# Expert weights of a block fetched by SyncE with the expert's number in a register, in place of an indirect transfer from GpSimd, with the order planned anew

## The chip, the cores and the metric

One core of a Trainium2 chip runs the kernel. Its engines are TensorE (PE for matmuls, PEld for weight loads), VectorE (DVE), ScalarE (ACT), GpSimd (POOL) and SyncE (SP), and 16 DMA engines move data for all of them. The metric is the device time in microseconds (us) of one execution; the times shown are medians over runs.

## The reference, cut to what matters

The input is 64 sequences of 128 tokens with 128 features, beside a context of 77 rows for each. Four layers follow one another: a transformer layer (self-attention, cross-attention, MLP), a layer with two attentions and a mixture of experts, a state-space block with cross-attention, and a last masked cross-attention with a norm. The change touches the mixture of experts alone:

```python
logits = h @ rw.T + rb                      # 8 experts
vals, idx = top_k(logits, 2)
gates = softmax(vals)
h1 = gelu(einsum('nd,efd->enf', hf, fc1_w) + fc1_b)   # D=128 -> FF=512, per expert
eo = einsum('enf,edf->end', h1, fc2_w) + fc2_b        # back to 128
mixed = (eo[idx, n] * gates).sum over the 2 chosen experts
return x + mixed
```

## The kernel before, in words

The 64 sequences are worked off in 16 passes of four sequences (NB = 4). Four streams (S = 4) are in flight at once, each with its own buffers; stream n does passes n, n+4, n+8 and n+12. A pass is a list of several hundred steps (`pass_steps`), each on one to three engines one after the other.

**What sets the order.** Every engine does its steps strictly in one order that is worked out before the kernel is built. `timetable` plays all four streams through with a length for each step (`parts`, in us, such as `"place": [(P, 0.9), (V, 5.0)]`), rules of priority (`EAGER`, `AHEAD`, `LEAD`, `STAY`) and a table `CHANGES` that overrides these rules for each stretch of planned time (`STRETCH`). Out of it come, for each engine, its list of steps (`pl.order`), the PSUM banks, and the order in which the passes hold the one set of expert slots (`pl.holders`). On the chip only this order counts: an engine that comes to a step waits on semaphores until its inputs are there, and everything behind it on that engine waits too.

**The mixture of experts.** The step `route` makes the logits, `pick` (L1655 to L1666, DVE) ranks them, `place` counts on PE (L1289 to L1293) and works out on DVE (L1674 to L1698) the row of each token in a list that is sorted by expert and padded to 15 blocks of 128 rows, and the expert of each block. `scatter` (L1850) writes the tokens to their rows in HBM with eight indirect DMAs from POOL. `sorted` (L1116, SP) reads the blocks back, `sort_turn` turns them. Then, for each of the 15 blocks j, `up` (L1307 on PE, L1705 on DVE, L1503 on ACT) and `down` (L1314 on PE, L1712 on DVE) use the weights in slot j % 4 of the tile `ew`. `put` (L1120, SP) writes the answers back, and `get` (L1869) gathers them with eight indirect DMAs from POOL.

**The weights of a block.** One expert is 128 rows of 4,624 bytes in the HBM tensor `experts`, 592 KB in all. `ew` has four slots. The step `fetch` (L1852 to L1863) is done 15 times a pass by POOL: it waits until `place` is done, and until the slot is free: for blocks 0 to 3 until the former holder's last `down`, from block 4 on until `down` of block j - 4. Then it issues an indirect DMA whose 128 row numbers stand in `expert_row`:

```python
g_.indirect_dma_start(ew[:, j % SLOTS, :], None, experts,
                      bass.IndirectOffsetOnAxis(expert_row[s][:, j:j + 1], 0))\
    .then_inc(experts_fetched[j % SLOTS], 16)
```

POOL also spreads the keys of every attention (L1880), works on every norm's statistics (L1811 to L1821), adds biases (L1840), and does parts of the state-space block. SP does nothing but wait and issue: `load` (L1095 to L1097), `context` (L1113), `sorted`, `put`, `store` (L1144).

Of the kernel before, what the change touches and what calls it, by code (L numbers as in the profile page):

```python
# [32 lines left out]
I32 = mybir.dt.int32  # L33
# [7 lines left out]
NE = 8  # L41
# [6 lines left out]
SLOTS = 4  # L48
# [159 lines left out]
def pe(n, count=1):  # L208

    return count * (0.006 + 0.00167 * n)  # L210
# [7 lines left out]
INDIRECT = 1.1  # L218


def parts(step):
# [50 lines left out]
    if kind == "out":  # L272
# [176 lines left out]
def timetable(streams):  # L449
# [106 lines left out]
    while True:  # L556
# [52 lines left out]
STRETCH = 80  # L609
CHANGES = [  # L610
    {"LEAD": 1.24415, "mix": {P: -0.7}},
    {"LEAD": 1.24415, "values": {P: 8.9, V: 0.5}, "soft": {V: 0.7}, "mix": {P: -0.7}, "pick": {V: -1.7},
     "scatter": {G: -3.8, Y: -3.8}, "scan": {V: -1.3}},
    {"LEAD": 1.24415, "STAY": 0, "values": {P: 8.9, V: 0.5}, "soft": {V: 0.7}, "mix": {P: -0.7}, "pick": {V: -1.7},
     "place": {V: 0.2}, "scatter": {G: -3.8, Y: -3.8}, "step_size": {P: 1.5}, "decay_in": {G: 20.8},
     "scan": {V: -1.3}, "gate_norm": {G: 2.7}},
    {"LEAD": 1.24415, "STAY": 0, "apply": {A: -0.6}, "values": {P: 8.9, V: 0.5}, "soft": {V: 0.7}, "mix": {P: -0.7},
     "pick": {V: -1.7}, "place": {V: 0.2}, "scatter": {G: -3.8, Y: -3.8}, "step_size": {P: 1.5},
     "decay_in": {G: 20.8}, "scan": {V: -1.3}, "gate_norm": {G: 2.7}},
    {"LEAD": 1.24415, "STAY": 7.88007854, "apply": {A: -0.6}, "values": {P: 8.9, V: 0.5}, "soft": {V: 0.7},  # L620
     "mix": {P: -0.7}, "pick": {V: -1.7}, "place": {V: 0.2}, "scatter": {G: -3.4, Y: -3.8}, "step_size": {P: 1.5},
     "decay_in": {G: 20.8}, "scan": {V: -1.3}, "gate_norm": {G: 2.7}},
    {"LEAD": 1.24415, "STAY": 2.24318536, "apply": {A: -0.6}, "values": {P: 8.9, V: 0.5}, "spread": {G: -1},
     "soft": {V: 0.7}, "turn": {P: 1.8, A: 1.8}, "mix": {P: -0.7}, "pick": {V: -1.7}, "place": {V: 0.2},
     "scatter": {G: -3.4, Y: -3.8}, "step_size": {P: 1.5}, "decay_in": {G: 20.8}, "scan": {V: -1.3},
     "gate_norm": {G: 2.7}},
    {"LEAD": 1.24415, "STAY": 2.24318536, "apply": {A: 1.7}, "values": {P: 8.9, V: 0.5}, "spread": {G: 0.7},
     "soft": {V: 0.7}, "turn": {P: 1.8, A: 1.8}, "mix": {P: -0.7}, "pick": {V: -1.7}, "place": {V: 0.2},
     "scatter": {G: -3.4, Y: -3.8}, "combine": {V: -1.4}, "step_size": {P: 1.5}, "decay_in": {G: 20.8},
     "scan": {V: -1.3}, "gate_norm": {G: 2.7}},  # L630
    {"LEAD": 1.24415, "STAY": 2.24318536, "apply": {A: 1.7}, "values": {P: 8.9, V: 0.5}, "spread": {G: 0.7},
     "soft": {V: 0.7}, "turn": {P: 1.8, A: 1.8}, "mix": {P: -0.7}, "pick": {V: -1.9}, "place": {V: 0.2},
     "scatter": {G: -3.4, Y: -3.8}, "combine": {V: -1.4}, "step_size": {P: 1.5}, "decay_in": {G: 20.8},
     "scan": {P: 6.5, V: 5.2, G: 5.3}, "gate_norm": {G: 2.7}},
    {"LEAD": 2.75006599, "bias_mlp": {G: -2.3}, "combine": {V: -2.2}},
    {"STAY": 7.7079338, "weigh": {G: -1.4}, "scan": {V: -1.2}},
    {"LEAD": 2.60550174, "STAY": 7.7079338, 5: 0.2, "apply": {A: -0.3}, "mlp": {V: 0}, "sort_turn": {P: 1.2, A: 1.9},
     "conv": {P: 1.1, V: 1.1, A: 1.2}, "weigh": {G: -1.4}, "scan": {V: -1.2}},
    {"LEAD": 2.60550174, "STAY": 7.7079338, 5: 0.2, "apply": {A: -0.3}, "mlp": {V: 0}, "sort_turn": {P: 1.2, A: 1.9},
     "conv": {P: 1.1, V: 1.1, A: 1.2}, "weigh": {G: -1.4}, "scan": {V: -1.2}, "mamba_out": {P: -3.7, V: -2.6}},  # L640
    {"LEAD": 2.60550174, "STAY": 7.7079338, 5: 0.2, "apply": {A: -0.3}, "mlp": {V: 0}, "place": {P: 1, V: 1},
     "sort_turn": {P: 1.2, A: 1.9}, "conv": {P: 1.1, V: 1.1, A: 1.2}, "weigh": {G: -1.4}, "scan": {V: -1.2},
     "gate_stats": {G: -0.1}, "mamba_out": {P: -3.7, V: -2.6}},
    {"LEAD": 2.60550174, "STAY": 1.47055777, 5: 0.2, "apply": {A: -0.3}, "mlp": {V: 0}, "place": {P: 1, V: 1},
     "sort_turn": {P: 1.2, A: 1.9}, "get": {Y: -1.2}, "conv": {P: 1.1, V: 1.1, A: 1.2}, "weigh": {G: -1.4},
     "scan": {V: -1.2}, "gate_stats": {G: -0.1}, "mamba_out": {P: -3.7, V: -2.6}},
    {"LEAD": 2.60550174, "STAY": 1.47055777, 5: 0.2, "apply": {A: -0.3}, "values": {P: 11.8}, "mlp": {V: 0},
     "place": {P: 1, V: 1}, "fetch": {G: -1.5, Y: -1.6}, "sort_turn": {P: 1.2, A: 1.9}, "get": {Y: -1.2},
     "step_size": {V: 5.1}, "conv": {P: 1.1, V: 1.1, A: 1.2}, "weigh": {G: -1.4}, "scan": {V: -1.2},
     "gate_stats": {G: -0.1}, "mamba_out": {P: -3.7, V: -2.6}},  # L650
    {"LEAD": 1.28926663, "STAY": 1.47055777, 5: 0.2, "apply": {A: -0.3}, "values": {P: 11.8}, "mlp": {V: 0},
     "place": {P: 1, V: 1}, "fetch": {G: -1.5, Y: -1.6}, "sort_turn": {P: 1.2, A: 1.9}, "get": {Y: -1.2},
     "step_size": {V: 5.1}, "conv": {P: 1.1, V: 1.1, A: 1.2}, "weigh": {G: -1.4}, "scan": {V: -1.2},
     "gate_stats": {G: -0.1}, "mamba_out": {P: -3.7, V: -2.6}},
    {"LEAD": 2.44299045, "STAY": 1.47055777, 5: 0.2, "apply": {A: -0.3}, "values": {P: 11.8}, "mlp": {V: 0},
     "place": {P: 1, V: 1}, "fetch": {G: -1.5, Y: -1.6}, "sort_turn": {P: 1.2, A: 1.9}, "get": {Y: -1.2},
     "step_size": {V: 5.1}, "conv": {P: 1.1, V: 1.1, A: 1.2}, "weigh": {G: -1.4}, "scan": {V: -1.2},
     "gate_stats": {G: -0.1}, "mamba_out": {P: -2.1, V: -2.6}},
    {"LEAD": 2.64227556, "STAY": 1.47055777, 5: 0.2, "apply": {A: -0.3}, "values": {P: 11.8}, "mlp": {V: 0},
     "place": {P: 1, V: 1}, "fetch": {G: -1.5, Y: -1.6}, "sort_turn": {P: 1.2, A: 1.9}, "get": {Y: -1.2},  # L660
     "step_size": {V: 5.1}, "conv": {P: 1.1, V: 1.1, A: 1.2}, "weigh": {G: -1.4}, "scan": {V: -1.2},
     "gate_stats": {G: -0.1}, "mamba_out": {P: -2.1, V: -2.6}},
    {"LEAD": 2.64227556, "STAY": 3.99262594, 5: 0.2, "apply": {A: -0.3}, "values": {P: 11.8}, "mlp": {V: 0},
     "place": {P: 1, V: 1}, "fetch": {G: -1.5, Y: -1.6}, "sort_turn": {P: 1.2, A: 1.9}, "get": {Y: -1.2},
# [1344 lines left out]
```

## Time and profile before

| | |
|---|---|
| median of 3 runs | 4012.08 us (4009.76 to 4013.83) |
| the profiled execution | 4007.73 us, its span 4005.9 us |
| mean granted clock of TensorE | 0.934 |
| busy: PE / DVE / ACT / POOL | 3432.5 / 2796.4 / 2686.8 / 1476.8 us |

An engine's busy time is the time in which it has an instruction of the program at work; waits, register work and the issuing of DMAs by SP are not counted. "remote", or "another core or an unknown queue", stands in this single-core trace where a semaphore came that no recorded instruction explains; "issue" is time in which an engine waited for nothing that the trace shows.

### The profile page before, as it was taken

Reading aid. Unit: us, or ns where it says so; the run is one execution under the profiler, and the core shown is the slowest. Engines: PE = TensorE matmul, PEld = TensorE weight load, DVE = VectorE, ACT = ScalarE, POOL = GpSimd, SP = SyncE. Lnnn points to the kernel's source line nnn. Section 1 sums busy time; section 2 is a strip of 40 time slices with the busy share of each in tenths; the row PEclk is TensorE's granted clock in tenths of the full one; section 3 lists DMA queues with packets and bytes.
Section 4 is the critical chain, followed back from the end, with each engine's and each line's share of the span. In section 5 each row is a group of like instructions: output and inputs, shape, how many; then the busy total and the mean of one; then the engine's idle time right before and its main releaser. Section 6 shows DMA issues by size and latency. Waiting matters only on the chain.

```text
span 4005.9 us, 86421 instructions
## 1 busy us (share of the span) xinstructions
PE 3432.5 (86%) x31600; PEld 2472.8 (62%) x31600; DVE 2796.4 (70%) x5826; ACT 2686.8 (67%) x4726; POOL 1476.8 (37%) x1844
## 2 busy tenths in 40 slices
PE   6888888889988979898988998988889798988776
PEld 3556656666656766575765765666566565756654
DVE  7777565757776766876767676776877667675554
ACT  3777665657867857696676766857667575767544
POOL 2123334434243343524334342343433425342441
PEclk9999998989999989999999989999899898999888
DMA  4000223121101221121111201221012211202210
GB/s 149 2 3 20 88 81 97 54 76 48 38 18 57 66 82 50 48 74 40 60 52 42 81 11 58 65 81 50 10 57 71 82 46 48 79 11 95 90 57 6
DMA packets 144378, 224.40 MB, mean 56 GB/s; under 512 B 20128, under 2 KB 106080, under 8 KB 143712
## 3 DMA queue, kind: packets, MB, share of 16 engines
q0 software_dynamic: 42752, 158.86, 12.4%
q1 hardware_dynamic: 101216, 60.02, 5.2%
q8 instruction: 265, 4.34, 0.5%
q14 instruction: 145, 1.19, 0.1%
HBM read 190.52 MB, written 36.98 MB: 57 GB/s over the span
## 4 chain that ended last, share of the span: by engine, by line
PE 49%; DVE 21%; ACT 13%; issue 6%; another core or an unknown queue 5%; POOL 3%; DMA 1%; SPq 1%; DVEq 0%; ACTq 0%; POOLq 0%
PE ps L1231 11%; PE ps L1243 6%; PE ps L1221 6%; DVE mx L1616 5%; DVE pr L1622 3%; ACT pt L1461 3%; PE ps L1307 3%; PE ps L1314 3%; PE ps L1190 3%; PE ps L1251 2%; PE ps L1216 2%; DVE kx L1755 2%; DVE kx L1622 2%; PE ps L1263 2%
## 5 line engine op out<-in xcount | busy, mean ns | idle before, releaser
L1616 DVE TENSOR_REDUCE mx<-ps 128x8 f32<-128x616 f32 (+1 forms) x704 | 671.5, 954 | 479.4 <-PE ps L1221 350.3
L1461 ACT ACTIVATE pt<-ps 77x512 f32<-77x512 f32 (+1 forms) x1408 | 769.4, 592 | 167.8 <-PE ps L1231 112.9
L1231 PE MATMUL ps<-k_sb,pr 128*77 128x128 f32 (+1 forms) x3776 | 564.6, 292 | 42.0 <-issue 12.4
L1231 PEld LDWEIGHTS ps<-k_sb,pr 128*77 128x77 f32 (+1 forms) x3776 | 442.5, 153 | 162.1 <-issue 98.9
L1243 PE MATMUL ps<-pt,v 77*16 77x128 f32 (+2 forms) x11264 | 471.1, 284 | 69.4 <-ACT pt L1461 33.7
L1452 ACT ACTIVATE pr<-pr 128x616 f32<-128x616 f32 (+1 forms) x472 | 394.8, 840 | 175.3 <-DVE pr L1622 165.4
L1880 POOL TENSOR_TENSOR kx<-kT,in_tiles 128x308 f32<-128x308 f32 (+1 forms) x384 | 317.4, 827 | 514.5 <-PE ps L1221 416.8
L1470 ACT ACTIVATE og<-ps 128x256 f32<-128x256 f32 x704 | 263.8, 377 | 299.1 <-PE ps L1243 174.2
L1622 DVE TENSOR_TENSOR pr<-ps,mx 128x616 f32<-128x616 f32 (+1 forms) x472 | 450.3, 954 | 16.2
L1221 PE MATMUL ps<-kx,qT 32*128 32x308 f32 (+2 forms) x2816 | 378.1, 570 | 82.4 <-ACT pt L1461 38.1
L1861 POOL DMA_INDIRECT ew<-experts,expert_row x240 | 238.8, 995 | 534.0 <-DVE kx L1712 440.1
L1243 PEld LDWEIGHTS ps<-pt,v 77*16 77x16 f32 (+2 forms) x11264 | 254.9, 99 | 275.1 <-issue 122.4
L1231 PE MATMUL ps<-k_sb,kx 128*77 128x128 f32 (+1 forms) x1856 | 280.4, 293 | 23.4 <-ACT og L1470 7.9
L1307 PE MATMUL ps<-pr,ew 128*128 128x128 f32 x1920 | 262.7, 281 | 23.0 <-DMA ew<-experts,expert_row 9.3
L1251 PE MATMUL ps<-k_sb,og 128*128 128x128 f32 x1408 | 234.7, 290 | 45.1 <-ACT og L1470 18.7
L1231 PEld LDWEIGHTS ps<-k_sb,kx 128*77 128x77 f32 (+1 forms) x1856 | 217.9, 153 | 85.8 <-issue 51.2
L1314 PE MATMUL ps<-ew,pt 128*128 128x128 f32 x1920 | 262.5, 281 | 8.7 <-ACT pt L1503 5.1
L1411 ACT ACTIVATE xh<-x,dt_p,rstd 128x128 f32<-128x128 f32 x448 | 183.9, 483 | 118.8 <-POOL dt_p L1821 118.7
L1307 PEld LDWEIGHTS ps<-pr,ew 128*128 128x128 f32 x1920 | 237.6, 194 | 41.7 <-issue 20.0
L1452 ACT ACTIVATE kx<-kx 128x616 f32<-128x616 f32 (+1 forms) x232 | 194.7, 840 | 100.9 <-DVE kx L1622 87.5
L1314 PEld LDWEIGHTS ps<-ew,pt 128*128 128x128 f32 x1920 | 236.9, 194 | 28.4 <-issue 16.5
L1251 PEld LDWEIGHTS ps<-k_sb,og 128*128 128x128 f32 x1408 | 164.7, 147 | 132.7 <-issue 53.1
(200 smaller groups left out, 6001.9 us busy)
## 6 DMA issues: line engine op xcount, KB each, us to landing
kx<-sorted_x SPq DMA_DIRECT2D x16, 960.0 KB, 9.1
sorted_y<-kx SPq DMA_DIRECT2D x48, 256.0 KB
x<-x SPq DMA_DIRECT2D x16, 256.0 KB, 3.2
experts<-weights SPq DMA_DIRECT2D x2, 2048.0 KB, 18.5
out<-xh SPq DMA_DIRECT2D x16, 256.0 KB, 2.5
sorted_x<-weights SPq DMA_DIRECT2D x4, 960.0 KB, 10.2
ew<-experts,expert_row POOLq DMA_INDIRECT x240
sorted_y<-kx SPq DMA_DIRECT2D x16, 192.0 KB
```

Of the source, the lines that this page charges most:

```text
L1221: i = mm(o, qT[s][r, b * L:(b + 1) * L], spread_keys[s][r, pl.slot(("spread", a, s, b), 2), 0:4 * keys], start=mask is None, stop=True)
L1231: i = tr(p[0:keys, j * L:(j + 1) * L], probs[s][pl.slot(unit, 3)][:, c:c + keys], ident)
L1243: i = mm(ps[32 * j:32 * j + t.slot, pl.banks[step][0], q * L:(q + 1) * L], heads_of(s, t)[0:keys, n, :], pt[s][0:keys, q, j * L:(j + 1) * ...
L1251: i = tr(p[:, q * L:(q + 1) * L], og[:, s % S, q * L:(q + 1) * L], ident)
L1307: i = mm(p[:, c * 128:(c + 1) * 128], E(j % SLOTS, "fc1", c * 128, (c + 1) * 128), blocksT[s][:, j * 128:(j + 1) * 128], start=True, stop= ...
L1314: i = mm(p[:, 0:D], h1[s][j % 2][:, c * 128:(c + 1) * 128], E(j % SLOTS, "fc2", c * D, (c + 1) * D), start=c == 0, stop=c == FC - 1)
L1452: go_act(v, v, ACT.Exp, scale=t.scale).then_inc(probs_ready.sem, 1)
L1461: go_act(pt[s][0:keys, q % 2, :], p[0:keys, :], ACT.Copy).then_inc(probsT_ready.sem, 1)
L1470: go_act(og[:, s % S, 2 * h * L:2 * (h + 1) * L], p[:, 0:2 * L], ACT.Copy)\
L1616: link(v_.tensor_reduce(m, tile, AX.X, ALU.max, negate=True))
L1622: tell(dve, v_.tensor_tensor(dst, tile, m.rearrange("p (c h) -> p c h", c=2).unsqueeze(3).broadcast_to([128, 2, 4, keys]), ALU.add), score ...
L1880: tell(pool, g_.tensor_tensor(spread_keys[s][:, pl.slot(step, 2), 0:4 * keys].rearrange("p (h k) -> p h k", h=4), kT[s][:, b * keys:(b + 1 ...
```

## The change

The step `fetch` goes from POOL to SP. `place` leaves the expert's number itself in a new tile `expert_id` in place of 128 row numbers. SP waits for the same four things as POOL did, loads the number from SBUF into a register, and issues an ordinary DMA whose source address is worked out from it. The tile `row_n` goes, with the one instruction that made it. In the planner, `fetch` is now one part on SP, the lengths of several steps are changed, `STRETCH` goes from 80 to 60, and `CHANGES` is a new table (60 stretches in place of 46), so the order of the steps on all five engines is a new one. No other instruction of the kernel differs.

```diff
-INDIRECT = 1.1
+INDIRECT = 1.03
...
     if kind == "fetch":
-        return [(G, INDIRECT), (Y, 3.4)]
+        return [(Y, 3.8)]
...
     if kind == "sorted":
-        return [(Y, 5.0)]
+        return [(Y, 7.5)]
     if kind == "put":
-        return [(Y, 3.0)]
+        return [(Y, 3.5)]
...
-        "pick": [(V, 1.9)], "place": [(P, 0.9), (V, 5.0)], "combine": [(V, 2.5)],
+        "pick": [(V, 2.5)], "place": [(P, 1.8), (V, 3.3)], "combine": [(V, 2.5)],
...
-        "up": [(P, pe(128, 4) + 0.02), (V, 0.72), (A, act(n))], "down": [(P, pe(D, 4) + 0.04), (V, 0.3)],
+        "up": [(P, pe(128, 4) + 0.07), (V, 0.72), (A, act(n))], "down": [(P, pe(D, 4) + 0.06), (V, 0.3)],
...
-STRETCH = 80
+STRETCH = 60
 CHANGES = [
...
@@ SyncE's steps
+                elif kind == "fetch":
+                    j = step[2]
+                    former = pl.holder(EXPERTS, s)
+                    sp.wait_ge(packed, 16 * 4)
+                    sp.wait_ge(*placed(s))
+                    if j >= SLOTS:
+                        sp.wait_ge(*down_ready(s, j - SLOTS))
+                    elif former is not None:
+                        sp.wait_ge(*down_ready(former, BLOCKS - 1))
+                    e = sp.value_load(expert_id[s][0:1, j:j + 1], min_val=0, max_val=NE - 1)
+                    sp.dma_start(ew[:, j % SLOTS, :], experts[bass.ds(e * 128, 128), :])\
+                        .then_inc(experts_fetched[j % SLOTS], 16)
@@ VectorE's preparation and the end of place
-            nc.vector.tensor_reduce(row_n[:], K("after"), AX.X, ALU.add)
...
-                    tell(dve, v_.scalar_tensor_tensor(expert_row[s][:], expert, 128.0, row_n[:].broadcast_to([128, BLOCKS]),
-                                                      ALU.mult, ALU.add), placed, s)
+                    tell(dve, v_.tensor_scalar(expert_id[s][:], expert, 0.0, None, ALU.add), placed, s)
@@ GpSimd's steps
-                elif kind == "fetch":
-                    s, j = args
-                    former = pl.holder(EXPERTS, s)
-                    pool.wait_ge(packed, 16 * 4)
-                    pool.wait_ge(*placed(s))
-                    if j >= SLOTS:
-                        pool.wait_ge(*down_ready(s, j - SLOTS))
-                    elif former is not None:
-                        pool.wait_ge(*down_ready(former, BLOCKS - 1))
-                    g_.indirect_dma_start(ew[:, j % SLOTS, :], None, experts,
-                                          bass.IndirectOffsetOnAxis(expert_row[s][:, j:j + 1], 0))\
-                        .then_inc(experts_fetched[j % SLOTS], 16)
```

## Rows read from the trace of the kernel before

**Rows 1.** The page: busy time of each engine, share of the span, instructions.
```profile
PE 3432.5 (86%) x31600; PEld 2472.8 (62%) x31600; DVE 2796.4 (70%) x5826; ACT 2686.8 (67%) x4726; POOL 1476.8 (37%) x1844
```

**Rows 2.** The page: the chain that ended last, share of the span by engine.
```profile
PE 49%; DVE 21%; ACT 13%; issue 6%; another core or an unknown queue 5%; POOL 3%; DMA 1%; SPq 1%; DVEq 0%; ACTq 0%; POOLq 0%
```

**Rows 3.** Busy time by stretch, sum of eight stretches without indirect DMAs, 658 us.
```profile
sum 658.00, PE 590.31 PEld 409.55 DVE 540.65 ACT 442.70 POOL 276.54; mean PE 73.79 PEld 51.19 DVE 67.58 ACT 55.34 POOL 34.57
```

**Rows 4.** The same, six stretches inside the work on blocks, 644 us.
```profile
sum 644.00, PE 603.13 PEld 451.99 DVE 481.18 ACT 514.67 POOL 238.61; mean PE 100.52 PEld 75.33 DVE 80.20 ACT 85.78 POOL 39.77
```

**Rows 5.** The same, eight stretches of 12 us from 4 us after a scatter's start, fetches behind.
```profile
sum 96.00, PE 40.75 PEld 26.28 DVE 33.01 ACT 21.58 POOL 73.81; mean PE 5.09 PEld 3.28 DVE 4.13 ACT 2.70 POOL 9.23
```

**Rows 6.** The same, nine stretches of 10 us from 4 us after a lone get's start.
```profile
sum 90.00, PE 49.84 PEld 30.48 DVE 27.66 ACT 26.93 POOL 50.25; mean PE 5.54 PEld 3.39 DVE 3.07 ACT 2.99 POOL 5.58
```

**Rows 7.** Timeline of all engines, 384 to 404 us: start, length, instruction, idle time before it.
```profile
384.76 1.23 POOL L1850 DMA_INDIRECT sorted_x<-xh,token_row  x1 [9.08 <-DVE expert_row L1698]
...
395.14 0.98 POOL L1861 DMA_INDIRECT ew<-experts,expert_row  x1 [0.30 <-issue]
...
397.69 0.80 DVE L1616 TENSOR_REDUCE mx<-ps 128x8 f32<-128x616 f32 x1 [6.90 <-remote]
...
402.01 0.38 ACT L1470 ACTIVATE og<-ps 128x256 f32<-128x256 f32 x1 [12.76 <-remote]
```

**Rows 8.** The tile `ew`: its fetch (ns min/median/max), and who waited for it (us, times).
```profile
L1861 POOL DMA_INDIRECT ew<-experts,expert_row x240: 932/979/1306, 395.1 to 3828.7; - x120
...
  PE ps L1307: 9.3, 9
```

**Rows 9.** Waits of all engines, us in total, times, longest.
```profile
POOL ew L1861 <- DVE kx L1712: 440.1, 100, 34.4
POOL kx L1880 <- PE ps L1221: 416.8, 93, 20.1
```

**Rows 10.** The longest pieces of the chain that ended last: start, length.
```profile
571.84 5.74 DMA ew<-experts,expert_row
...
2003.10 6.75 DMA ew<-experts,expert_row
...
2228.32 4.42 DMA ew<-experts,expert_row
```

**Rows 11.** DMA queues (packets, MB, share) and issues (count, KB, us to landing).
```profile
q8 instruction: 265, 4.34, 0.5%
...
kx<-sorted_x SPq DMA_DIRECT2D x16, 960.0 KB, 9.1
...
w_sb<-weights SPq DMA_DIRECT2D x1, 1280.0 KB, 9.7
...
k_sb<-consts SPq DMA_DIRECT2D x1, 366.0 KB, 3.0
```

**Rows 12.** SP's waits: the DMA it held back, who ended it, total, times, longest.
```profile
SPq L1120 <- DVE kx L1712: 1684.0, 64, 60.6
SPq L1113 <- PE ps L1221: 874.2, 16, 205.6
```

**Rows 13.** Timeline of POOL, 523 to 562 us, the first fetches of pass 1.
```profile
524.67 0.98 POOL L1861 DMA_INDIRECT ew<-experts,expert_row  x1 [5.35 <-DVE kx L1712]
...
529.18 0.95 POOL L1869 DMA_INDIRECT pr<-sorted_y,token_row  x1 [0.30 <-issue]
...
544.38 0.98 POOL L1861 DMA_INDIRECT ew<-experts,expert_row  x1 [0.27 <-POOL kx L1880]
```

**Rows 14.** Timeline of DVE, 1190 to 1199 us: first and last of `pick`, of `place`.
```profile
1189.91 0.43 DVE L1660 TENSOR_TENSOR tmp<-lg 128x256 f32<-128x256 f32 x1
...
1192.08 0.18 DVE L1666 TENSOR_SCALAR chosen<-rank 128x32 f32<-128x32 f32 x1
...
1194.42 0.19 DVE L1674 TENSOR_TENSOR tmp<-chosen,ex 128x32 f32<-128x32 f32 x1 [0.85 <-DVE mv L1575]
...
1198.15 0.17 DVE L1698 SCALAR_TENSOR_TENSOR expert_row<-tmp,row_n 128x15 int32<-128x15 f32 x1
```

More of the change, by code:

```diff
@@ new lines @@
+    {"LEAD": 2.50676729, "STAY": 1.16629123, "load": {V: -1.6}, "stats": {G: 2.4}, "values": {P: 9.4},
+     "mix": {P: -0.2}, "regroup": {P: 2.2, V: 2.2}, "bias_mlp": {G: 0.1}, "mlp": {V: -2.6}, "context": {Y: -1.4},
+     "route": {A: -0.4}, "pick": {V: 0.2}, "place": {V: -3}, "sorted": {Y: -2.5}, "down": {P: -0.1, V: 0.8},
+     "put": {Y: 1.7}, "combine": {V: -2.1}, "step_size": {A: 1}, "decay_in": {G: 17}, "decay": {P: -0.1, A: -0.1},
+     "pairs": {P: -2.7, V: -3.8}, "weigh": {G: 2.2}, "rows": {V: 3.4}, "gate_stats": {V: 0.4, G: 1.2},
+     "mamba_out": {V: -2.5}},
@@ new lines @@
+    {"LEAD": 1.96836201, "STAY": 1.16629123, "load": {V: -1.6}, "stats": {G: 2.4}, "values": {P: 9.4},
+     "mix": {P: -0.2}, "regroup": {P: 2.2, V: 2.2}, "bias_mlp": {G: 0.1}, "mlp": {V: -2.6}, "context": {Y: -1.4},
+     "route": {A: -0.4}, "pick": {V: 0.2}, "place": {V: -3}, "sorted": {Y: -2.5}, "down": {P: -0.1, V: 0.8},
+     "put": {Y: 1.7}, "combine": {V: -2.1}, "step_size": {A: 1}, "decay_in": {G: 17}, "decay": {P: -0.1, A: -0.1},
+     "pairs": {P: -2.7, V: -3.8}, "weigh": {G: 2.2}, "rows": {V: 3.4}, "gate_stats": {V: 0.4, G: 1.2},
+     "mamba_out": {V: -2.5}},
@@ new lines @@
+    {"LEAD": 1.96836201, "STAY": 1.42654065, "load": {V: -1.6}, "stats": {G: 2.4}, "values": {P: 9.4},
+     "mix": {P: -0.2}, "regroup": {P: 2.2, V: 2.2}, "bias_mlp": {G: 0.1}, "mlp": {P: -3.4, V: -2.6},
+     "context": {Y: -1.4}, "route": {A: -0.4}, "pick": {V: 0.2}, "place": {V: -3}, "sorted": {Y: -2.5},
+     "down": {P: -0.1, V: 0.8}, "put": {Y: 1.7}, "combine": {V: -2.1}, "step_size": {A: 1}, "decay_in": {G: 17},
+     "decay": {P: -0.1, A: -0.1}, "pairs": {P: -2.7, V: -3.8}, "weigh": {G: 2.2}, "rows": {P: 4.5, V: 7.9},
+     "gate_stats": {V: 0.4, G: 1.2}, "mamba_out": {V: -2.5}},
@@ new lines @@
+    {"LEAD": 1.96836201, "STAY": 1.36940616, "load": {V: -1.6}, "stats": {G: 2.4}, "rope": {V: -2.5},
+     "values": {P: 9.4}, "mix": {P: -0.2}, "regroup": {P: 2.2, V: 2.2}, "bias_mlp": {G: 0.1},
+     "mlp": {P: -3.4, V: -2.6}, "context": {Y: -1.4}, "route": {A: -0.4}, "pick": {V: 0.2}, "place": {V: -3},
+     "sorted": {Y: -2.5}, "down": {P: -0.1, V: 0.8}, "put": {Y: 1.7}, "get": {G: 4.3, Y: 4.3}, "combine": {V: -2.1},
+     "step_size": {A: 1}, "conv": {A: -0.4}, "decay_in": {G: 17}, "decay": {P: -0.1, A: -0.1},
+     "pairs": {P: -2.7, V: -3.8}, "weigh": {G: 2.2}, "rows": {P: 4.5, V: 7.9}, "gate_stats": {V: 0.4, G: 1.2},
+     "gate_norm": {G: 0.3}, "mamba_out": {V: -2.5}},
@@ new lines @@
+    {"LEAD": 1.32647018, "STAY": 1.36940616, 0: 0.2, "load": {V: -3.7, Y: -2.1}, "stats": {G: 2.4},
+     "rope": {V: -2.5}, "values": {P: 9.4}, "mix": {P: -0.2}, "regroup": {P: 2.2, V: 2.2}, "bias_mlp": {G: 0.1},
+     "mlp": {P: -3.4, V: -2.6}, "context": {Y: -1.2}, "route": {A: -0.4}, "pick": {V: 0.2}, "place": {V: -3},
+     "scatter": {Y: 1.7}, "sorted": {Y: -0.9}, "down": {P: -0.1, V: 0.8}, "put": {Y: 1.7}, "get": {G: 4.3, Y: 4.3},
+     "combine": {V: -2.1}, "step_size": {P: 2.6, A: 1}, "step_size2": {V: 0.8}, "conv": {A: -0.4},
+     "decay_in": {G: 17}, "decay": {P: -0.1, A: -0.1}, "pairs": {P: -3.5, V: -4.6}, "z": {A: 1}, "weigh": {G: 2.2},
+     "rows": {P: 4.5, V: 7.9}, "scan": {G: 1.6}, "gate_stats": {V: 0.4, G: 1.2}, "gate_norm": {G: 0.3},
+     "mamba_out": {P: -0.6, V: -2.6}},
@@ L722 @@
+    {"soft": {A: 1.9}, "out": {P: -0.8}},
 ]
@@ L891, in build @@
         token_row = Ring([sb(f"token_row{s}", [128, 2, NB], I32) for s in range(S)])
-        expert_row = Ring([sb(f"expert_row{s}", [128, BLOCKS], I32) for s in range(S)])
+        expert_id = Ring([sb(f"expert_id{s}", [128, BLOCKS], I32) for s in range(S)])
         ones = sb("ones", [128, 128])
```

429 lines of the change are left out of this document (317 added, 112 removed).

## The prediction

> **What bounds the kernel now.** I read the page's busy times first: TensorE is at work for 3432.5 of 4005.9 us, the others for 70% or less, POOL for 37% [rows 1]. So TensorE's work is the floor, and the 573 us in which it has no matmul are all that can be won here, since no matmul is removed. The chain that ended last says who holds it up: PE itself 49%, DVE 21%, ACT 13%, but POOL only 3%, DMA 1%, and a share of 5% (about 200 us) of unknown origin [rows 2]. POOL, from which the change takes work, is hardly ever the one that is waited for. Next I split the idle time by stretch. Away from the mixture of experts TensorE is busy for 590.31 of 658 us, 89.7% [rows 3]; in the work on blocks for 603.13 of 644, 93.7% [rows 4]; but from 4 to 16 us after a scatter starts for 40.75 of 96, 42% [rows 5], and after a lone get for 49.84 of 90, 55% [rows 6]. The timeline shows what those holes look like: POOL issues eight scatters from 384.76 and four fetches from 395.14 on, and DVE gets its next input only at 397.69 after 6.90 us, ACT at 402.01 after 12.76 us, both marked remote [rows 7]. TensorE's own share falls in just these stretches [rows 5, 6]. That happens around runs of indirect DMAs from POOL and makes up much of the unknown 5%.
>
> **What the change does, part by part.**
>
> *A. POOL loses its issues.* 240 indirect DMAs at a median of 979 ns, 235 us of busy time [rows 8]. Also POOL stood 440.1 us at a fetch whose slot was not free [rows 9], with key spreads, norm statistics and biases queued behind it. Little of that counts: POOL has 3% of the chain (120 us) against 1476.8 us of work, so 8% of its work lies on the path, and 8% of 235 us is 19 us. Bounds: nothing, and twice that (38) if the work queued behind blocked fetches was what the chain met. I take 19. The waits of 440.1 us are not added: key spreads wait a similar 416.8 us for TensorE anyway [rows 9], so POOL is ahead of its readers.
>
> *B. Shorter runs of indirect DMAs.* Each pass has one run of eight scatters and one of eight gets, which stay. The first four fetches of a pass mostly hang on one of them and stretch it by four issues at about 1.28 us (0.98 and the 0.30 before it, [rows 7]), 5 us. With fetches behind, TensorE is busy for 42%, without for 55% [rows 5, 6]: 13 points of 12 us, 1.6 us a pass, 25 us for 16. Bounds: nothing, if it is the bytes and not POOL's issuing that hurt; and 16 times 5.1 us at the idle share of 58%, 47 us. I take 25.
>
> The Trainium skill (Runtime: NRT & Kernel Launch, Instruction fetch mechanics) says that each sequencer fetches its instructions in 16 KiB blocks over a DMA queue of its own. The trace agrees as to the blocks: 265 packets with 4.34 MB on the instruction queue [rows 11]. By that rule a hole would be a late block; if what delays it are the expert bytes, which stay the same, B is 0 and my sum is 25 us less of a gain.
>
> *C. How late a block's weights are.* On POOL a fetch on the chain takes 4.42 to 6.75 us from issue to the matmul's release, about 4.4 where it is undisturbed [rows 10]. For SP I interpolate between ordinary loads: 366 KB in 3.0 us, 1280 KB in 9.7 us [rows 11], 7.3 ns a KB, so 4.6 us for 592 KB less about nothing for longer rows. The transfer itself gains nothing. New is the register load, which no row shows; it can cost nothing beside the wait before it, or at most what the costliest thing in the path costs now, an issue of POOL, 1 us. I take 1 us, and 1.2 us later in all. All but a few fetches have cover: a slot is asked for three blocks ahead, and TensorE waited only 9.3 us in 9 cases [rows 8]. If cover is short in one fetch of 20 to 40, that is 6 to 12 times 1.2 us, 8 us lost. Bounds: 0 and 15. Against this, the first four no longer queue with POOL's other runs: in pass 1 three fetches went from 524.67 on, eight gets came between, and the fourth went at 544.38 [rows 13], 20 us late. That shortens the time for which a pass holds the slots, and is worth something only through the order, in D.
>
> The Trainium skill (DMA: Bandwidth & Descriptors, Latency and other measured facts) puts the floor of a tensor_load at about 600 ns. With that in place of 1 us, C would be 5 us and not 8.
>
> *D. The new order.* It is the largest unknown, as all five engines get another one. What the trace can test are the lengths it was planned with. `pick` takes 2.4 us on DVE from 1189.91 to 1192.26 (planned 1.9, now 2.5), `place` 3.9 us from 1194.42 to 1198.32 (5.0, now 3.3) [rows 14]; the return of the sorted blocks lands after 9.1 us [rows 11] (5.0, now 7.5). These come nearer. Against them, an indirect DMA costs POOL 1.28 us in a run (1.1, now 1.03): 2 us too little for a run of eight. The errors put right are a few us in a pass of about 1000 us (four in flight, 4000 us), so they can't move much by themselves. But a plan made on them, with the experts' slots free of POOL's queue, can pack TensorE better where it is at 89.7% beside 93.7% inside the work on blocks. I take one point of the four over some 3,200 us (4006 less 32 holes of 12 us and about 400 us of ramp and tail): 32 us gained. Bounds: three points (96 us), and one point in the other direction (32 us lost), since an order is as easily worse by that much as better.
>
> *E. The rest costs nothing.* The last instruction of `place` is 0.17 us [rows 14] and is replaced by one of the same size, and `row_n` was made once at the start, under the first loads. Five or so register and wait instructions on SP for each fetch run on an engine that does nothing else; they matter only as in C. SP's queue is the real matter, below.
>
> **The sum.** The profiled execution took 4007.7 us, 1.8 us more than its span and 4.4 us less than the median. 19 + 25 - 8 + 32 = 68 us: 3939.7 in the profiled execution, 3944 beside the median of 4012.1.
>
> **The rivals.**
>
> *R1: SP becomes the queue in which everything waits (slower).* Until now SP could stand anywhere without harm: 1684.0 us before puts, 874.2 us before context loads, one of them for 205.6 us [rows 12]. Now 240 fetches stand in that same line. A context load waits for another stream's scores; where the plan put it just ahead of a fetch and those scores are late by a hole of 7 to 13 us [rows 7], the fetch is late by as much. Cover is three blocks. It decides from the point where SP is later than that: TensorE is in order too, so an `up` without weights stops all four streams. One such stop of 6 us a pass is 96 us; less the gains of A and B (44) and with D and C at nothing that is 4064, at 3 us a pass 4016. I put its middle at 4040. For it: the long waits of SP. Against it: the order of SP is planned with these same steps, and POOL was in order too and cost only 9.3 us.
>
> *R2: only the issuing moves (no change).* The same bytes move at the same moments, so the holes stay as they are and B is nothing; the order gives nothing; A less C is 11 us, and the time 4001, or up to 4012 if A is nothing too. For it: POOL's 3% of the chain [rows 2]. Against it: 42% beside 55% in the runs [rows 5, 6]. The Trainium skill has this as a rule (DMA: Bandwidth & Descriptors, Issuing engines are not separate DMA queues): all issuers share 16 DMA engines, and another one saves only the sequencer's time.
>
> *R3: the freed slots and the order give much more.* D at its bound of 96 us and B at 47: 4012 - 19 - 47 - 96 + 8 = 3858; half way from my forecast, 3900. For it: where a pass waits for the slots, as pass 1 in [rows 13], a fetch at once shortens its path. Against it: latency is mostly hidden by four streams.
>
> **How the numbers follow.** Forecast (3915 to 3985) 0.45; R3 0.22; R2 (within or just beyond the edge of no change) 0.14; R1, with an order that is simply worse, 0.19. A measurement of this kernel can tell 0.2% (8 us) from no change. R2 is split between same and just faster: faster 0.72, same 0.10, slower 0.18. The range leaves out the far half of R3 below 3875 and the far part of R1 above 4035.
>
> **What would show it.** A: POOL's busy time near 1240 us, and L1861 gone. B: in runs of eight scatters TensorE's share from 4 to 16 us rises from 42% towards 55%; if it stays, the bytes or the runs themselves are the cause. C: from the end of SP's issue to the matmul's release 4 to 5 us, and TensorE's waits for `ew` at 10 to 25 us in total. D: stretches without experts at 90 to 92% for TensorE. R1 would show as waits of TensorE at L1307 on the DMA of `ew` of 50 us and more, with SP standing before a context load or a put while a slot was free. I am wrong if the span falls with TensorE's share unchanged in the holes and outside, or if L1307's waits carry the loss.

## The result, and the profile after

The changed kernel takes 3917.5 us (3914.2 to 3923.8, four runs) where the kernel before takes 4013.0 beside it: ratio 0.9751, 95% interval 0.971 to 0.979, so 95 us less. The forecast was 3944 us, 68 us less. The profiled execution took 3919.1 us, its span is 3917.3, TensorE's mean granted clock 0.938. Busy times and the chain that ended last, of the page after, beside [rows 1] and [rows 2]:

```profile
PE 3414.8 (87%) x31600; PEld 2472.8 (63%) x31600; DVE 2801.1 (72%) x5825; ACT 2692.0 (69%) x4732; POOL 1236.9 (32%) x1604
...
PE 53%; DVE 19%; ACT 13%; issue 6%; another core or an unknown queue 4%; POOL 3%; DMA 2%; SPq 1%; ACTq 0%; DVEq 0%; POOLq 0%
```

POOL has 240 us less to do, TensorE 18. POOL's 3% of the chain has not moved: by the chain alone, its 240 us were worth nearly nothing. The share of unknown origin falls from 5% to 4%.

The weights, by tile `ew` and by the register load's line (ns min/median/max; then who waited for the transfer, us and times), beside [rows 8]:

```profile
L1363 SPq DMA_DIRECT2D ew<-experts x240: 3/338/996, 387.0 to 3746.9; - x120
...
  DMA ew<-experts: 6.5, 7
```

```profile
L1362 SPq TENSOR_LOAD <-expert_id x240: 16/268/1061, 386.0 to 3746.2; - x120
L1362 SPq FUSED_REGOPS  x240: 148/152/193, 386.5 to 3746.5; - x120
```

The whole of SP's work for a fetch is a load of 0.27 us, register work and an issue of 0.34 us. TensorE waits 6.5 us for weights in the whole kernel, 9.3 before. The longest pieces that the weights have in the chain that ended last (start, length), beside [rows 10]:

```profile
605.99 3.76 DMA ew<-experts
...
1732.72 3.90 DMA ew<-experts
...
2668.17 4.54 DMA ew<-experts
```

They were 4.42 to 6.75 us and are 3.76 to 4.54. The records of the packets say where this comes from (medians). Over the 176 fetches that need a `down` of their own pass, it is 5.4 us before and 4.5 after from the end of that `down` to the last packet. From the issue's start to the last packet it is 4.4 us before and 3.8 after, and the first packet comes 1.8 us after POOL began an issue and 0.95 after SP did. Where the `down` was what the engine waited for, it issues 0.8 us behind it either way, on SP with the register load in these 0.8 us.

SP's waits (the DMA held back, who ended it, total, times, longest), beside [rows 12]; L1359 is a fetch behind a `down`, L1361 the first of a pass, L1352 the context, L1371 `put`:

```profile
SPq L1359 <- DVE kx L1961: 1128.4, 157, 48.4
...
SPq L1361 <- DVE expert_id L1948: 674.9, 12, 89.5
SPq L1352 <- PE ps L1472: 481.4, 16, 209.0
SPq L1371 <- DVE kx L1961: 310.4, 33, 24.7
```

SP still stands before a context load for up to 209 us. Of the 176 fetches, three go out 3.9 to 9.8 us behind their `down`, two of them because SP waited to issue a `store` and the third in line behind the second. None of the three is late for a context load.

Now the stretches. TensorE from 4 to 16 us after the start of each of the 16 runs of scatters, sum of 192 us, kernel before, then after:

```profile
sum 192.00, PE 89.48 PEld 60.70 DVE 74.72 ACT 53.28 POOL 128.59; mean PE 5.59 PEld 3.79 DVE 4.67 ACT 3.33 POOL 8.04
```

```profile
sum 192.00, PE 116.83 PEld 76.44 DVE 84.35 ACT 75.05 POOL 112.49; mean PE 7.30 PEld 4.78 DVE 5.27 ACT 4.69 POOL 7.03
```

47% becomes 61%. Eight stretches of the kernel after without experts and indirect DMAs, and eight inside the work on blocks, beside [rows 3] and [rows 4]:

```profile
sum 680.00, PE 600.79 PEld 419.30 DVE 566.61 ACT 435.40 POOL 299.01; mean PE 75.10 PEld 52.41 DVE 70.83 ACT 54.43 POOL 37.38
```

```profile
sum 667.00, PE 644.33 PEld 512.82 DVE 494.81 ACT 585.83 POOL 135.61; mean PE 80.54 PEld 64.10 DVE 61.85 ACT 73.23 POOL 16.95
```

88% without experts, where 90 to 92% was forecast, and 96.6% inside the blocks, 93.7% before (each run's stretches are picked from its own timeline). The changed kernel packs the block work, not the rest.

### The profile page after: what moved, and what is told of

Its sections match the earlier page's. It is cut to its first block, busy times and chain, and to the rows that moved or that the text cites. A ratio compares the mean times of both kernels' runs of the same rounds, so it can differ in the third digit from the quotient of the medians.

```text
span 3917.3 us, 87600 instructions
## 1 busy us (share of the span) xinstructions
PE 3414.8 (87%) x31600; PEld 2472.8 (63%) x31600; DVE 2801.1 (72%) x5825; ACT 2692.0 (69%) x4732; POOL 1236.9 (32%) x1604
## 3 DMA queue, kind: packets, MB, share of 16 engines
q8 instruction: 265, 4.34, 0.5%
q14 instruction: 154, 1.26, 0.1%
## 4 chain that ended last, share of the span: by engine, by line
PE 53%; DVE 19%; ACT 13%; issue 6%; another core or an unknown queue 4%; POOL 3%; DMA 2%; SPq 1%; ACTq 0%; DVEq 0%; POOLq 0%
PE ps L1482 12%; PE ps L1494 6%; PE ps L1472 6%; DVE mx L1866 4%; ACT pt L1712 4%; PE ps L1558 4%; PE ps L1565 4%; PE ps L1502 3%; DVE pr L1872 3%; PE ps L1441 3%; PE ps L1467 2%; PE ps L1514 2%; PE ps L1613 2%; DVE kx L1872 1%
## 5 line engine op out<-in xcount | busy, mean ns | idle before, releaser
L1482 PE MATMUL ps<-k_sb,pr 128*77 128x128 f32 (+1 forms) x3776 | 554.9, 289 | 42.4 <-ACT pt L1712 16.4
L1482 PEld LDWEIGHTS ps<-k_sb,pr 128*77 128x77 f32 (+1 forms) x3776 | 434.1, 151 | 159.2 <-issue 86.7
L1472 PE MATMUL ps<-kx,qT 32*128 32x308 f32 (+2 forms) x2816 | 368.0, 556 | 56.5 <-ACT pt L1712 28.7
L2089 POOL TENSOR_TENSOR x<-x,r_sb 128x512 f32<-128x512 f32 x96 | 122.9, 1280 | 423.4 <-PE ps L1425 358.4
L2067 POOL TENSOR_SCALAR dt_p<-mv 128x4 f32<-128x4 f32 (+1 forms) x144 | 35.0, 243 | 679.3 <-DVE mv L1825 677.4
```

Source lines behind the costliest of these rows:

```text
L1472: i = mm(o, qT[s][r, b * L:(b + 1) * L], spread_keys[s][r, pl.slot(("spread", a, s, b), 2), 0:4 * keys], start=mask is None, stop=True)
L1482: i = tr(p[0:keys, j * L:(j + 1) * L], probs[s][pl.slot(unit, 3)][:, c:c + keys], ident)
```

## The experiments

They ran on four chips of two kinds, and that became a finding of its own. On chip 2 (called A here) the kernel before takes 4013.8 us. On the chips 11, 5 and 9 it takes 3771, 3773 and 3777 us; they behaved alike and are together called B. The chip of the two kernels' runs above isn't on record, and their times are like A's. Each ratio is to the kernel before on the same chip, and only ratios are compared across chips.

| kernel | chip | us | ratio to before | 95% interval |
|---|---|---|---|---|
| move alone | A (2) | 3921.6 | 0.9766 | 0.9742 to 0.979 |
| order alone | A (2) | 3981.2 | 0.9911 | 0.9886 to 0.9936 |
| move, tiny issues left on POOL | A (2) | 4030.0 | 1.0042 | 1.0028 to 1.0056 |
| change, runs spaced by filler | A (2) | 4007.0 | 0.998 | 0.9964 to 0.9997 |
| move, POOL's waits left | B (11) | 3735.2 | 0.9903 | 0.9883 to 0.9923 |
| the same and 1.2 us of work | B (11) | 3777.7 | 1.0008 | 0.9988 to 1.0029 |
| change, runs split and replanned | B (11) | 3991.6 | 1.0589 | 1.0561 to 1.0616 |
| change, runs woven | B (11) | 3702.4 | 0.982 | 0.9798 to 0.9842 |
| the change itself | B (5) | 3695.3 | 0.98 | 0.9784 to 0.9815 |
| change, runs woven, again | B (5) | 3705.7 | 0.9824 | 0.981 to 0.9838 |
| move alone, again | B (9) | 3731.5 | 0.9883 | 0.9863 to 0.9903 |
| order alone, again | B (9) | 3766.6 | 0.9972 | 0.996 to 0.9984 |

**Move alone.** The kernel before with its old order on every engine; only the fetch stands in SP's branch, at the place that its transfer had in the plan, and `place` writes `expert_id`.

```diff
-                elif kind == "fetch":              # POOL
-                    ...
-                    g_.indirect_dma_start(ew[:, j % SLOTS, :], None, experts, ...)
+                elif kind == "fetch":              # SP
+                    ...
+                    e = sp.value_load(expert_id[s][0:1, j:j + 1], min_val=0, max_val=NE - 1)
+                    sp.dma_start(ew[:, j % SLOTS, :], experts[bass.ds(e * 128, 128), :])
```

> The order of before on all five engines, step for step, with SyncE issuing the fetches where the old plan has their transfer. Theory M (the move does it: POOL's issues off the path, shorter runs of indirect DMAs): half or more of the 95 us is here, 3950 to 3970, and TensorE's share from 4 to 16 us after a scatter starts rises from 42% to over 50%. Theory O (the new order does it): 3995 to 4012, the holes as before. Rival R1 (SyncE's line blocks): above 4020, with TensorE waiting 50 us and more for the weights.

92 us of the 95 on chip A, more than either theory had. The move is by itself nearly the whole gain there. Of the 86 us between the two profiled executions, 44 are idle time of TensorE (515 us in place of 559, weight loads counted as work). The rest is shorter matmuls, 3391.4 us in place of 3432.5: by the records of the granted clock TensorE is at the lower of its two levels (1.2 GHz) for 438 us in place of 529.

**Order alone.** The changed kernel's order on all engines, and the fetches as indirect DMAs on POOL, put in at their planned moments.

```diff
+        fetches = [step for step in self.order[Y] if step[0] == "fetch"]
+        self.order[G] = sorted(self.order[G] + fetches,
+                               key=lambda step: self.begins[step][Y if step[0] == "fetch" else G])
```

> The order of after on all five engines, with POOL issuing the fetches by indirect DMA at the moment that the new plan has for them. Theory M: 3965 to 3990, only the order's share. Theory O: 3920 to 3940. If the new order counts on a POOL without fetches it may lose much of its gain here, above 3990.

33 us, as the theory of the move had it. The parts sum to 125 us, the whole is 95: they overlap. Its waits of TensorE for weights (total, times, longest) against the 6.5 us after the change:

```profile
PE ps L1550 <- DMA ew<-experts,expert_row: 47.2, 36, 4.4
```

The new order spends the cover that the old one had for slow fetches.

**The issues without the bytes.** The move alone, and at a fetch's old place POOL does the same waits and an indirect DMA of 4 bytes a row, which nothing reads.

```diff
+                    g_.indirect_dma_start(probe[:, tries[0] % 30, :], None, small,
+                                          bass.IndirectOffsetOnAxis(expert_row[s][:, j:j + 1], 0))
```

> As the move alone, but POOL also issues, where before had the fetch and with the same waits, an indirect DMA of 4 bytes a row into a small spare tile (it adds work; the output is as before). If POOL's issuing and its waits cost what the move won, the time is that of before, 4000 to 4012, and the holes are back at 42%. If it was the 592 KB by indirect DMA that hurt, it stays within 8 us of the move alone.

All of the gain is gone and 16 us more. The bytes of the weights still move, by SP; what came back are POOL's waits and issues. (Some of the 16 us are its own: POOL waits 44 us for earlier ones of these small transfers.) TensorE in the 16 stretches behind a scatter's start, move alone and then with the tiny issues:

```profile
sum 192.00, PE 106.34 PEld 71.10 DVE 75.73 ACT 68.54 POOL 104.37; mean PE 6.65 PEld 4.44 DVE 4.73 ACT 4.28 POOL 6.52
```

```profile
sum 192.00, PE 75.40 PEld 49.69 DVE 59.46 ACT 40.59 POOL 126.65; mean PE 4.71 PEld 3.11 DVE 3.72 ACT 2.54 POOL 7.92
```

55% without issues behind the run, which is the number forecast for it, and 39% with them. The sums hide how clean this is. In the kernel before, four fetches follow at once behind nine of the 16 runs, and two or fewer behind the other seven, in the same order of steps. TensorE's share behind the nine is 40% before, 59% with the move alone and 31% with the tiny issues. Behind the seven it is 55%, 50% and 50%. Behind the runs of gets nothing is won: 53% from 4 to 14 us over all 16 before, 48% with the move alone, 51% with the change.

**Runs spaced by filler.** The changed kernel, and behind each scatter and each get three small multiplications on POOL, which turn an interval of 1.26 us into 2.68.

```diff
+                            for _ in range(3):
+                                link(g_.tensor_tensor(scratch[:], k_sb[:, 0:128], k_sb[:, 0:128], ALU.mult))
```

> After, with three small multiplications of POOL's behind each of the 16 scatter and get DMAs of a pass (they add some 1.2 us between two issues). If the holes come from indirect DMAs issued back to back, TensorE's share in the first 16 us of a run goes from about 50% to over 75%, and the time falls to 3850 to 3900 though POOL has some 380 us more of work. If each indirect DMA costs TensorE its share however they are spaced, the holes get longer and flatter and the time is 3915 to 3945.

The time is 62 us and more above what either expectation had. The chain that ended last has no unknown share any more, and POOL in its place:

```profile
PE 44%; DVE 19%; POOL 16%; ACT 10%; issue 7%; DMA 3%; SPq 1%; DVEq 0%; POOLq 0%; ACTq 0%
```

TensorE's signals are in time now (last section), and its share is 93% from 4 to 14 us behind a get's start and 70% from 4 to 16 us behind a scatter's, short of the 75% expected. A run that occupies POOL for 21 us costs all that the holes had cost and 90 us more. So there are two costs of a run, late signals and an occupied POOL. The next runs fell on B, where no signal is late, and so show the second by itself.

**Waits alone, waits with work.** Both are the move alone; at a fetch's old place POOL does its four waits and issues nothing, and in the second also three multiplications.

```diff
+                elif kind == "fetch":              # POOL, both
+                    ...
+                    pool.wait_ge(*down_ready(s, j - SLOTS))
+                    for _ in range(3):             # the second only
+                        link(g_.tensor_tensor(scratch[:], k_sb[:, 0:128], k_sb[:, 0:128], ALU.mult))
```

> The run with before's order and the fetches on SyncE (3921.6 us), with this one addition: at the place of each fetch GpSimd waits for what the fetch waited for (the expert number in place, the slot of the weights free) and issues nothing. With an issue of almost no bytes at that place the time was 4030.0 us. Theory Q (the waits block GpSimd's queue: pick, kx and the next run of transfers stand behind them): most of the 108 us comes back, 3990 to 4030 us. Theory R (the issue itself lengthens a run of indirect transfers, in which TensorE's signals come late): next to nothing comes back, 3920 to 3940 us, and the share of TensorE 4 to 16 us behind a scatter's start stays at the 55% of the moved kernels. In between, 3945 to 3985 us, both hold a part, and the parts are read off it.

> As the run with the waits alone, and behind each wait GpSimd does three small multiplications, about 1.4 us of work in place of an indirect issue of about 1 us, with no transfer. Theory Q (GpSimd's queue: waiting and being occupied) has the same 4000 to 4040 us as with the empty issue, since the engine is occupied as long. Theory R (what counts is that the issue is an indirect transfer in a run of them, which delays TensorE's signals) has it at most 20 us above the run with the waits alone, below 3990 us.

The waits alone have 0.9903 on chip 11 and the move alone 0.9883 on chip 9: 8 us less by the medians of the ratios, and the intervals overlap. POOL standing at a fetch costs little or nothing. The work brings the time back to that of the kernel before. It is this row, and the chain that ended last of the first and of the second:

```profile
L1872 POOL TENSOR_TENSOR scratch<-k_sb 128x128 f32<-128x128 f32 x720 | 290.1, 403 | 441.7 <-DVE kx L1722 394.0
```

```profile
PE 53%; DVE 22%; ACT 13%; issue 5%; POOL 4%; DMA 1%; SPq 1%; DVEq 0%; ACTq 0%; POOLq 0%
```

```profile
PE 51%; DVE 20%; ACT 13%; POOL 8%; issue 6%; DMA 1%; SPq 1%; DVEq 0%; POOLq 0%; ACTq 0%
```

290 us of work on POOL, spread over 240 places, cost 42 us, 15% of it. No transfer is needed for this. Neither chain has an unknown share. The expectations were in times of chip A. As ratios to the kernel before there, the run with the work lies where theory Q had it and above theory R, and the run with the waits lies between the two. So of theory Q the occupied engine holds and the waiting does not. On chip A the waits alone were not run.

**Runs split, runs woven.** In the first the planner gets each scatter and get as eight steps and orders everything anew with the same table. In the second only POOL's order changes: the steps planned within 6 us behind a run go between its pieces.

```diff
-    out += norm_steps(6, s) + [("route", s), ("pick", s), ("place", s), ("scatter", s)]
+    out += norm_steps(6, s) + [("route", s), ("pick", s), ("place", s)] + [("scatter", s, n) for n in range(2 * NB)]
```

```diff
+            until = self.begins[step][G] + dict(parts(step))[G] + 6.0
+            while steps and len(behind) < 2 * NB - 1 and steps[0][0] not in ("scatter", "get") \
+                    and self.begins[steps[0]][G] <= until:
+                behind.append(steps.pop(0))
```

> The changed kernel with each scatter and each gather of eight indirect transfers given to the planner as eight steps of one transfer, so that it places other steps of GpSimd between them and orders everything anew; the table of lengths is not fitted to it. If GpSimd's back-to-back runs are the cause of the stretches in which TensorE's signals come late, those stretches shrink, TensorE's share 4 to 16 us behind a scatter's start rises above 60%, and the time falls to 3880 to 3915 us if the new order is as good as the old. If the stretches come of the amount of indirect issues and not of their spacing, the share stays near 55% and the time is 3915 to 3960 us. A planner's order that is worse for other reasons would show as idle time of TensorE outside these stretches.

> The changed kernel with the order of every engine but GpSimd kept; only GpSimd's own order is changed: the steps that the plan has within 6 us behind a run of eight indirect transfers are put between its pieces. Spacing by real work instead of filler. If the late signals of a back-to-back run are what idles TensorE there, 3890 to 3912 us; if a later end of the runs costs as much as the stretches did (as with the filler, 4007 us, where a run took some 20 us), 3915 to 3950 us.

Split, it is 6% slower than the kernel before, with signals in time and only 17.5 us of waits for weights. TensorE is idle for 582 us, the change on chip 5 for 368, so what it lost is the order. The table was made for the old steps; an order that isn't made for its steps costs 296 us against the change, by times of two chips of kind B. Woven, nothing was to be had on B, where no signal is late.

**The change itself and the woven one, side by side.**

> The changed kernel unaltered, a second time, beside the one whose transfers are woven into other work of GpSimd. The four runs before this one stood on another chip than the first four: there the kernel before takes 3770.7 us in place of 4013.8 us at equal durations of VectorE's, ScalarE's and GpSimd's instructions, and TensorE's signals are late by 0.02 us at most times, where the first chip shows up to 4 us behind a run of eight indirect transfers. Theory L (the move's gain came mainly of these late signals): where the kernel before takes about 3771 us the ratio is 0.985 to 0.995, 3715 to 3752 us; where it takes about 4013 us it is 0.975 again. Theory Q (GpSimd's blocked queue is the larger part): the ratio is 0.975 to 0.980 on either chip, 3676 to 3695 us on the one of 3771 us.

> The woven order of GpSimd a second time, beside the changed kernel itself. Where signals are late (before at about 4013 us), theory L has it 10 to 60 us below the changed kernel, 3860 to 3910 us, since no run of eight stands alone; where they are not (before at about 3771 us), it repeats 3702 us, ratio 0.982, and is within 10 us of the changed kernel, since there is nothing for it to cure. A time above the changed kernel by 10 us or more on either chip would say that the later end of the runs costs more than their spacing saves.

Both ran on chip 5, of kind B. The change keeps 2.0% of its 2.5% where no signal is late, at the edge of theory Q's range and outside theory L's: most of its gain does not need late signals. The woven one is 10 us above it, just where the later end of its runs was to count, but the two intervals overlap, so that is not decided. Whether weaving pays on chip A, where it was meant to, wasn't measured.

**The two parts on B.**

> The move alone (before's order on every engine, the fetches on SyncE) a second time, for the chip on which the kernel before takes about 3771 us, the changed kernel 3695 us, the move with GpSimd's waits left in 3735 us and with waits and 1.4 us of work 3778 us. If GpSimd's queue is the larger part of the gain there too, the move alone has 3690 to 3710 us (ratio 0.979 to 0.984), and 25 to 45 us of the 77 us are the waits, the rest the occupied engine. If the gain there is the new order's, the move alone stays near the run with the waits, 3725 to 3745 us (0.988 to 0.993). Where the kernel before takes about 4013 us, 3921 us again.

> The order alone (the changed kernel's order on every engine, the fetches as indirect transfers on GpSimd) a second time. On the chip of 4013 us it gave 36 us of the 95 us, and the move alone 92 us. If the two overlap because both take GpSimd's transfers out of each other's way, the order alone gives 20 to 45 us here too (3726 to 3751 us at 3771 us before) and the two parts sum to more than the whole; if its gain there came only of the late signals, it is within 10 us of the kernel before.

Move alone 44 us and order alone 11 on chip 9, together 75 on chip 5: here the whole is more than the parts, on chip A it was less. The first expectation missed: the move alone lies where the new order was to be the gain, and the order alone gives next to nothing. By itself neither is the whole gain on B. TensorE's waits for weights with the order alone, then with the move added (us, times, longest):

```profile
PE ps L1550 <- DMA ew<-experts,expert_row: 59.8, 40, 5.1
```

```profile
PE ps L1558 <- DMA ew<-experts: 6.4, 6, 2.4
```

The 53 us of waits between the two are enough for the missing 20 us; how many of them reach the end of the kernel isn't shown. Inside the work on blocks TensorE's share is 94.1% with the move alone, 94.0% with the order alone and 96.6% with both (94.2, 94.4 and 96.6% on chip A): what the order packs there needs the faster fetch.

## Why the prediction was right, point by point

Direction and most of the size came out: 3917.5 us lies in the likeliest case's own range (3915 to 3985), at its lower edge, 27 us below the forecast. Of the terms, two (A and B) were about half of what they are, one (C) was a loss that did not come, and one (D) was right alone and wrong in a sum. That the sum came as near is in part luck: A and B were short by some 40 us together, and D, taken on top of the move, was too large by 28.

*The floor.* "TensorE's work is the floor", with 573 us of idle time as all that can be won, did not hold. With the same 31,600 matmuls TensorE is busy for 3432.5 us before, 3391.4 with the move alone and 3313.5 with the change on chip 5, and its granted clock is at the lower level for 529, 438 and 212 us of these executions. The prediction had no term for the clock, and on chip A nearly half of the move's gain is in it.

*A, POOL loses its issues: forecast 19 us (0 to 38), measured some 34 to 44.* The step that failed is "8% of its work lies on the path". With 290 us put back, 42 us came back, 15%; by that rate 235 us are 34 us, with the waits 42, and the move alone has 44 us on B, where no signal is late. The 8% were read from a chain with 5% of unknown origin. In the run with the waits alone, whose chain has no unknown share, POOL has 4%, about 149 us against 1241.5 us of work. That is 12%, or 35 of the 42 us. So the share that was read was about half of the rate measured, and a share read where no part of the chain is unknown comes near that rate. The rate itself was measured on B alone. That the 440.1 us of waits needn't be added was right: what they cost, 8 us at the medians, can't be told from nothing.

*B, shorter runs: forecast 25 us (0 to 47), right in kind, about half in size.* 42% to 55% was forecast for the stretch behind the scatters. Over all 16 the move alone shows 47% to 55%, 17 us more of TensorE's work, and more than all of it stands behind the nine runs with four fetches at once behind them (40% to 59%). What the move gives on chip A beyond B is 48 us, the upper bound. It is a difference between chips, and the lower clock after a hole is in it, so it bounds B and doesn't measure it. The bytes were the other explanation. It fell: with tiny issues and SP's transfers the share is 39%. By the Trainium skill (Runtime: NRT & Kernel Launch, Instruction fetch mechanics) a sequencer fetches its instructions in blocks of 16 KiB, and the prediction made of it that a hole could be a late block. No run supports that: the instruction queue has the same 265 packets of 4.34 MB on chip 5, and no hole, and with the change on A the 44 instruction packets around the runs (from 2 us before the start to 16 behind) take 0.95 us at the median and 2.0 at most, the others 0.93 and 2.2. When the sequencer asked for them is in no record.

*C, how late the weights are: forecast 1.2 us later and 8 us lost, measured 0.9 us earlier and nothing lost that shows.* Both halves of the step failed. The register load was priced by an issue of POOL (1 us) and is 0.27 us, and in all SP issues no later behind a `down` than POOL did. The transfer was taken as equal, and the time from the issue's start to the first packet (1.8 us on POOL, 0.95 on SP) was left out. The Trainium skill (DMA: Bandwidth & Descriptors, Latency and other measured facts) has a floor of about 600 ns for such a load; the trace's median of 268 ns is below it, and the measurement decides. TensorE's waits, forecast at 10 to 25 us, are 6.5.

*D, the new order: forecast 32 us, measured 33 alone on chip A, 11 alone on B, and 4 and 31 to 36 on top of the move (the last across chips 9 and 5).* As a number by itself it was right, as a term of a sum it was not: it was added to A and B as if independent. On chip A both parts shrink the same holes: TensorE is at 47% behind a scatter's start before, 55% with the move, 63% with the order (120.6 of 192 us), 61% with both. How much of the overlap that is, no run shows. On B there are no such holes (82 to 87%), and the order needs the faster fetch. The place was wrong too: not the stretches without experts, which stay at 88 to 90%, but the blocks, 93.7% to 96.6%.

*E* cost nothing that shows. *R1, SP's line:* SP stands before a context load for up to 209 us as before, and TensorE waits 6.5 us for weights where the rival wanted 50; four streams and three blocks of cover are enough. *R2, only the issuing moves:* it was right that only the issuing moved, with the same bytes, and wrong in both prices: that gave 92 us on chip A, where the holes did not stay as they were, and 44 on B, where there are none. The rule behind it in the Trainium skill (DMA: Bandwidth & Descriptors, Issuing engines are not separate DMA queues), that this saves only the sequencer's time, holds for what is saved; here that time was worth it. *R3* wanted 3900 us, with A at its 19 and D at 96; the time lies between it and the forecast, and neither of these terms came.

## What to carry to other kernels

Price work that is taken off an engine that runs in order by putting the same occupation back as filler with no transfer. The engine's share of the chain is a first estimate, and a low one where the chain has a part of unknown origin: 8% was read here and 15% measured, on another chip. Two edits can relieve the same stretch and give less than their sum, and an order planned for a faster step can need that step and give more: test each alone before their gains are summed. A chip can have a share in a gain, as the move's 2.3% on A and 1.2% on B; take the ratio on a second one before a cause is believed.

## What the hardware showed that was not expected

The same program, the changed kernel, has a span of 3917.3 us in the first measurement (like chip A's, and called so here) and 3693.5 on chip 5. VectorE, ScalarE and GpSimd take the same time for each instruction (954 ns, 592 ns, 818 ns for the costliest groups on both). The page's busy times on chip 5:

```profile
PE 3313.5 (90%) x31600; PEld 2413.1 (65%) x31600; DVE 2802.8 (76%) x5825; ACT 2685.2 (73%) x4732; POOL 1238.0 (34%) x1604
```

The 224 us are two things of about the same size. TensorE is idle, with its weight loads counted as work, for 368 us in place of 490, and this difference sits behind POOL's runs of indirect DMAs: in the first 16 us of the 32 runs it is idle for 50 us in place of 173. And its matmuls are 101 us shorter, at a mean granted clock of 0.971 in place of 0.938. By the clock's records it is at the lower level for 212 us in place of 489, and 24 and 225 of these lie in the same first 16 us. The timeline of chip A from POOL's last scatter on (start, length, instruction, idle time before it), then chip 5's from its own:

```profile
395.96 0.96 POOL L2099 DMA_INDIRECT sorted_x<-xh,token_row  x1 [0.30 <-issue]
...
397.03 0.38 ACT L1721 ACTIVATE og<-ps 128x256 f32<-128x256 f32 x1 [5.10 <-remote]
...
398.52 1.08 ACT L1712 ACTIVATE pt<-ps 77x512 f32<-77x512 f32 x2 [1.11 <-remote]
...
400.71 0.80 DVE L1866 TENSOR_REDUCE mx<-ps 128x8 f32<-128x616 f32 x1 [10.16 <-PE ps L1472]
```

```profile
394.29 0.96 POOL L2099 DMA_INDIRECT sorted_x<-xh,token_row  x1 [0.31 <-issue]
...
397.83 1.22 DVE L1866 TENSOR_REDUCE mx<-ps 128x8 f32<-128x1024 f32 x1 [2.82 <-PE ps L1472]
...
398.33 0.39 ACT L1721 ACTIVATE og<-ps 128x256 f32<-128x256 f32 x1 [2.57 <-PE ps L1494]
398.96 1.08 ACT L1712 ACTIVATE pt<-ps 77x512 f32<-77x512 f32 x2 [0.24 <-PE ps L1482]
```

"remote" is TensorE here. Its semaphores move later than its matmuls end by the records: by 0.02 us nearly everywhere, but on chip A by 0.7 us at 2 to 4 us after a run's start, by 1.7 and 3.2 us in the next two steps of 2 us, by 4.0 at 10 to 12 us, about when the run of eight ends, and by 0.02 again from 14 us on (means over all runs of the kernel after). In the spaced run on chip A it is about 0.1 us or less, and on B it is 0.02 us behind the same back-to-back runs. VectorE's, ScalarE's and GpSimd's signals move 0.01 us behind their instructions, there too.

The signals do not only come late, they come together. In the kernel after, all 32 runs taken together, TensorE gives 1 to 21 signals in each us from 2 to 11 us behind a run's start, 98 in the us from 11 to 12, and 39 to 50 in every one of these on chip 5. The run's last issue ends at 10 us. The kernel before shows what four fetches more do: behind the nine runs that have them at once behind, the last issue ends at 15 us and the burst is at 17 to 18 us (23 signals for nine runs). With the move alone it is at 11 to 12 us again, and with the tiny issues at 17 to 18. So on chip A the end of the run sets when TensorE's signals come, and the fetches on POOL put that end off by 5 us; this is term B at work. The 16 stretches behind a scatter's start on chip 5:

```profile
sum 192.00, PE 166.33 PEld 116.52 DVE 145.10 ACT 127.10 POOL 135.49; mean PE 10.40 PEld 7.28 DVE 9.07 ACT 7.94 POOL 8.47
```

87% in place of 61%, with the same eight issues at the same 1.26 us. So a back-to-back run of indirect issues isn't enough to make TensorE's signals late; it takes chip A as well, and no other of the four numbered chips showed it. What differs between the chips stays open, as does whether the late thing is the signal itself or the recorded end of a matmul that in truth ended later.
